# A perceiver kernel on one core: the second cross attention with transposed scores, f32r values and a LayerNorm folded into its weights

## The chip, the cores and the metric

The kernel runs on one core of a Trainium2 chip, as one program that holds a two-layer perceiver. The metric is the device time of one execution in microseconds (us), the median of several. PE is TensorE, DVE VectorE, ACT ScalarE, POOL GpSimd, SP the engine whose queue issues the DMAs.

## What is computed

Sixteen sequences of 64 latent vectors of width 128 (1024 rows) pass two layers. The part that the change touches is the cross attention of layer 1, cut to what matters:

```python
x = x + xattn(ctx_1024, layernorm(x), ln1_w, ln1_b, ln2_w, ln2_b, Wq, Wkv, Wo)

def xattn(ctx, latents, ...):            # ctx (16, 1601, 128), latents (16, 64, 128)
    xn   = layernorm(ctx) * ln1_w + ln1_b
    latn = layernorm(latents) * ln2_w + ln2_b
    q    = latn @ Wq                     # 16 heads of 64
    k, v = split(concat([xn, latn], axis=1) @ Wkv)
    w    = softmax(q k^T / 8)            # (16, 16 heads, 64, 1665)
    return (w v) @ Wo
```

Everything is f32. Kernels of this case compute a product of f32 numbers in two ways. One is TensorE's f32 product, which shows as two records. The other splits each operand into a high half rounded to f32r and a low half (the rest, as f32r), and adds three f32r passes: high by high, high by low, low by high.

## The kernel before, in words

The program runs in stages, one block of instructions after another: the cross attention of layer 0 (tensor names `a_`), the folding of the weights of the second cross attention (`f_`), the rest of layer 0 (`b_`), the second cross attention (`c_`) and the rest of layer 1 (`d_`). A block begins when all engines have ended the one before, and the DMAs of it.

**Folding** (`fold_resampler_weights`, L1064). For each of 16 heads the query and key weights become one 128 by 128 matrix `qk`, the value and output weights one matrix `wvo`. TensorE transposes the raw blocks, then multiplies them, and DVE and ACT copy the results from PSUM. ln2's affine is applied to the latents in the rest of layer 0, ln1's to the context in the attention.

**Rest of layer 0** (`rest_of_layer_0`, L1130). Two rounds (a `Fori`) of four tiles, each tile two sequences. At its end TensorE makes the absorbed queries: in two parts (L1296) eight heads of `qk` by the transposed latents of each tile, which ACT and DVE copy out of PSUM and SP stores in DRAM (`absorbed_queries`, 512 KB a sequence). So 16 heads by 64 latents form 1024 columns a sequence.

**Second cross attention** (`attend`, L114, driven by `cross_attention_1`, L1745). A batch is one sequence: 1665 keys (1601 of context in 12 tiles of 128 and one of 65, and 64 of latents as the fourteenth tile, all side by side in one row) by 1024 queries. It is taken as 8 pairs of heads (128 queries), four pairs to a quad. For each pair the scores come with queries as partitions and keys as columns, in four chunks of up to 512 keys, three f32r passes each (L266). DVE takes the maximum of each chunk from PSUM (L359) and the largest of the four. ACT computes exp of the chunks with that maximum as bias and adds up the rows on the way (L340). TensorE transposes the probabilities (L237), DVE (L369, L373) and ACT (L324) copy them to SBUF, and when a quad is complete they are multiplied by the normalised rows `c_xn` in f32 (L1904, 512 columns). The reciprocal of the sums is spread over 128 partitions by a diagonal that POOL makes (L1918), and TensorE (`norm`). DVE multiplies the values by it; one f32 product per head with `wvo` makes the output of two sequences (L1890), which DVE adds to `x_tok`.

In the course of a batch the next one is prepared: DVE takes the statistics of its context, POOL computes the root (L1827, a power), normalises 13 tiles of rows (L1836), applies ln1's weight and bias (L1843, L1850) and splits the queries into halves (L1820, L1822). TensorE transposes the rows (L1884), ACT takes the high half of the result (L1939) and DVE the low half (L1946). A table places each of these jobs in one of 16 slots of a body of two sequences; every engine works through its list in order and waits on semaphores.

## Time and profile before

| | us |
|---|---|
| median of 3 runs | 2067.46 (2066.22 to 2070.15) |
| the profiled execution | 2070.69 |
| its span in the trace | 2068.9 |
| busy: PE 1746.9, DVE 1276.0, ACT 853.5, POOL 504.4 | 84%, 62%, 41%, 24% |
| second cross attention, between its first and last score | 966.6 |

The profiled execution is 1.8 us longer than its span, since it counts what lies around the first and the last instruction. It is 3.2 us above the median. The granted clock of TensorE, averaged over the span, was 0.909 of full speed.

### The profile page before, as it was taken

Reading aid. Unit: us, or ns where it says so; the run is one execution under the profiler, and the core shown is the slowest. Engines: PE = TensorE matmul, PEld = TensorE weight load, DVE = VectorE, ACT = ScalarE, POOL = GpSimd, SP = SyncE. Lnnn points to the kernel's source line nnn. Section 1 sums busy time; section 2 is a strip of 40 time slices with the busy share of each in tenths; the row PEclk is TensorE's granted clock in tenths of the full one; section 3 lists DMA queues with packets and bytes.
Section 4 is the critical chain, followed back from the end, with each engine's and each line's share of the span. In section 5 each row is a group of like instructions: output and inputs, shape, how many; then the busy total and the mean of one; then the engine's idle time right before and its main releaser. Section 6 shows DMA issues by size and latency. Waiting matters only on the chain. (4 is left out here: it accounts for less than half of the span.)

```text
span 2068.9 us, 33746 instructions
## 1 busy us (share of the span) xinstructions
PE 1746.9 (84%) x11837; PEld 1232.3 (60%) x11837; DVE 1276.0 (62%) x3092; ACT 853.5 (41%) x1895; POOL 504.4 (24%) x684
## 2 busy tenths in 40 slices
PE   5899999999966666428999999999999999999432
PEld 2466666666655555426666666766667666675322
DVE  5566666666736545636666656666666666654467
ACT  2355555565532122114444444444444444443132
POOL 1000001000001010023442344443234444320133
PEclk9699999999977776768999999999999999999765
DMA  4344435444210020040000000000000000000000
GB/s 104 92 105 105 112 81 113 98 112 106 55 42 1 1 81 0 0 152 27 27 11 27 16 26 26 26 10 26 18 23 26 26 26 10 16 1 1 0 5 5
DMA packets 32628, 90.06 MB, mean 44 GB/s; under 512 B 8552, under 2 KB 17424, under 8 KB 32528
## 3 DMA queue, kind: packets, MB, share of 16 engines
q1 hardware_dynamic: 32528, 88.71, 16.0%
q8 instruction: 65, 1.06, 0.2%
q14 instruction: 35, 0.29, 0.0%
HBM read 40.43 MB, written 8.91 MB: 24 GB/s over the span
## 5 line engine op out<-in xcount | busy, mean ns | idle before, releaser
L1904 PE MATMUL c_pv_ps<-c_prob_t,c_xn 128*128 128x512 f32 (+2 forms) x896 | 413.1, 598 | 0.0
L340 ACT ACTIVATE c_prob<-c_score_ps,c_neg_max 128x512 f32<-128x512 f32 (+1 forms) x512 | 304.3, 607 | 60.4 <-PE c_scratch L1890 35.0
L871 DVE TENSOR_REDUCE a_chunk_max<-a_side_ps 128x1 f32<-128x512 f32 (+1 forms) x416 | 260.7, 664 | 109.5 <-PE a_side_ps L692 109.4
L359 DVE TENSOR_REDUCE c_chunk_max<-c_score_ps 128x1 f32<-128x512 f32 (+1 forms) x512 | 290.9, 581 | 38.1 <-PE c_score_ps L266 36.6
L237 PE MATMUL c_turn_ps<-consts,c_prob 128*128 128x128 f32 (+2 forms) x1792 | 285.7, 276 | 5.2 <-DVE c_prob_t L369 4.3
L237 PEld LDWEIGHTS c_turn_ps<-consts,c_prob 128*128 128x128 f32 (+2 forms) x1792 | 212.4, 139 | 89.2 <-issue 32.4
L1904 PEld LDWEIGHTS c_pv_ps<-c_prob_t,c_xn 128*128 128x128 f32 (+2 forms) x896 | 158.4, 191 | 164.6 <-issue 164.5
L373 DVE COPY c_prob_t<-c_turn_ps 65x128 f32<-65x128 f32 (+1 forms) x256 | 61.5, 280 | 300.5 <-PE c_turn_ps L237 300.5
L804 ACT ACTIVATE a_prob<-a_st_ps 128x1024 f32<-128x1024 f32 (+1 forms) x224 | 214.4, 958 | 66.8 <-PE a_st_ps L676 66.8
L266 PE MATMUL c_score_ps<-c_x_hi,c_q_hi 128*128 128x512 f32 (+1 forms) x512 | 218.8, 427 | 2.4 <-ACT c_prob L340 1.6
L266 PE MATMUL c_score_ps<-c_x_hi,c_q_lo 128*128 128x512 f32 (+1 forms) x512 | 188.6, 368 | 0.0
L324 ACT ACTIVATE c_prob_t<-c_turn_ps 128x512 f32<-128x512 f32 x128 | 76.4, 597 | 270.7 <-PE c_turn_ps L237 269.2
L266 PE MATMUL c_score_ps<-c_x_lo,c_q_hi 128*128 128x512 f32 (+1 forms) x512 | 187.6, 366 | 0.0
L369 DVE COPY c_prob_t<-c_turn_ps 128x512 f32<-128x512 f32 x256 | 173.8, 679 | 0.2 <-PE c_turn_ps L237 0.2
L676 PE MATMUL a_st_ps<-a_q_bd,a_stack 100*128 100x256 f32 (+1 forms) x832 | 167.5, 320 | 0.0
L692 PE MATMUL a_side_ps<-a_stack,a_q_bd 96*128 96x512 f32 (+1 forms) x512 | 155.2, 389 | 3.6 <-DVE a_chunk_max L871 1.3
L1913 POOL CAST c_rden_hi<-c_rden 128x4 fp32r<-128x4 f32 x32 | 6.0, 187 | 529.3 <-DVE c_rden L383 529.3
L725 PE MATMUL a_pv_ps<-a_prob,a_val 128*17 128x128 f32 (+1 forms) x3328 | 134.3, 276 | 0.7 <-ACT a_raw L829 0.4
L676 PEld LDWEIGHTS a_st_ps<-a_q_bd,a_stack 100*128 100x128 f32 (+1 forms) x832 | 115.0, 187 | 29.7 <-issue 26.8
L1939 ACT ACTIVATE c_x_hi<-c_scratch 128x512 fp32r<-128x512 f32 x64 | 33.2, 518 | 191.1 <-PE c_scratch L1884 191.1
L725 PEld LDWEIGHTS a_pv_ps<-a_prob,a_val 128*17 128x17 f32 (+1 forms) x3328 | 71.7, 96 | 62.3 <-issue 58.5
L266 PEld LDWEIGHTS c_score_ps<-c_x_hi,c_q_lo 128*128 128x128 f32 x512 | 97.8, 191 | 17.4
(286 smaller groups left out, 2649.9 us busy)
## 6 DMA issues: line engine op xcount, KB each, us to landing
a_stack<-a_k_hi SPq DMA_DIRECT2D x128, 200.1 KB, 4.1
a_stack<-a_k_lo SPq DMA_DIRECT2D x64, 200.1 KB, 4.2
a_ctx<-in_ctx_dram SPq DMA_DIRECT2D x16, 768.0 KB
c_ctx<-in_ctx_dram SPq DMA_DIRECT2D x16, 768.0 KB
absorbed_queries<-b_q_out SPq DMA_DIRECT2D x16, 512.0 KB, 4.7
c_q_raw<-absorbed_queries SPq DMA_DIRECT2D x16, 512.0 KB, 3.3
w<-in_L_ffn_w_dram SPq DMA_DIRECT2D x2, 512.0 KB
f_raw<-in_L_xattn_Wkv_dram SPq DMA_DIRECT2D x2, 512.0 KB, 4.7
```

The costliest lines, as they stand in the source:

```text
L237: last = nc.tensor.transpose(turn_ps[c % 2][0:rows, P * i:P * i + P], prob[(s - 1) % 2][:, col:col + rows], ident)
L266: mm = nc.tensor.matmul(score_ps[:, cols], queries, keys_t[:, cols], start=(i == 0), stop=(i == len(passes) - 1))
L324: nc.scalar.activation(prob_t[u][:, 8:12, P * j:P * j + P], turn_ps[0][:].rearrange("p (t q) -> p t q", t=4), ACT.Copy).then_inc(copied_ac ...
L340: nc.scalar.activation(prob[s % 2][:, cols], score_ps[:, cols], ACT.Exp, bias=neg_max[:, s % 2:s % 2 + 1], accum_out=sums[:, (s // QUAD) % ...
L359: nc.vector.reduce_max(chunk_max[:, s % 2, c:c + 1], score_ps[:, quad_chunk(c, keys)], AX_X).then_inc(chunk_max_done, 1)
L369: last = nc.vector.tensor_copy(prob_t[u][:, 4 * c:4 * c + 4, P * j:P * j + P], turn_ps[c][:].rearrange("p (t q) -> p t q", t=4))
L676: last = nc.tensor.matmul(st_ps[t % 2][0:rows, i, 256 * v:256 * v + 256], stack[:, m, 2 * u + v, col:col + rows], q_bd[m][:, 2 * u + v].re ...
L692: return nc.tensor.matmul(out, q_bd[m][0:ONES_AT, v, 2 * (j % 2):2 * (j % 2) + 2, :].rearrange("p h q -> p (h q)"), stack[0:ONES_AT, m, v, ...
L725: last = nc.tensor.matmul(pv_ps[32 * j:32 * j + V_COLS, 0:P], val[m][0:rows, 2 * s + i, QUAD * u + j, :], prob[t % 3][0:rows, i, P * j:P * ...
L804: nc.scalar.activation(out, scores, ACT.Exp).then_inc(exp_done, 1)
L871: nc.vector.reduce_max(out, rows, AX_X).then_inc(side_taken, 1)
L1904: last = nc.tensor.matmul(lay.own.pv_ps[:], t.xn[m][0:rows, i, :], lay.own.prob_t[u][0:rows, i, :], start=(i == 0), stop=(i == LAT))
```

## The change

- **Folding.** The LayerNorm affines go into the weights. `qk` and `wvo` hold two matrices for each head, one for context keys and one for latent keys. The 16 transposes of the key and value blocks become 16 products of 256 columns with `fold_k` or `fold_v`, and for each head there is one product of 256 columns and two of 128. DVE and ACT share the copies in four banks. Four more small DMAs load the vectors.
- **Rest of layer 0.** The two rounds are written out without the `Fori`. The normalised rows are not copied to `heads_t` by DVE, the next operation reads them where they are. The absorbed queries are made in four parts instead of two, stored in two tensors of the old size.
- **Second cross attention**, written anew. A batch is two octets of eight heads (512 queries), an octet has seven steps of two key tiles: the same 14 tiles, but the latents have their own queries (those folded with their own affine) and columns set apart in the rows. For each key tile the scores come transposed, with keys as partitions and 512 queries as columns, in three f32r passes; the tile of latents has a fourth with one row. Since a maximum over keys can't be taken there, it comes from separate products of one pass with queries as partitions (`max_units_of_c`, 14 to an octet, in two banks, an octet and more ahead); DVE reduces them, and four tiny transposes bring the shift into row 0 of `q_lo`, so that the scores' product subtracts it. ACT takes exp of 128 by 1024 and then writes the high half of the result; DVE, or POOL at steps 1 and 4, the low half. The values are three f32r passes for each key tile with `v_hi` and `v_lo` as weights; POOL splits the values. Column 0 of the rows holds ones, so that row 0 of the result is the sum. The probabilities are not transposed or copied. `norm` is preceded by eight one-row products (`den`), and the output takes 32 products for two sequences instead of 16.
- POOL's list is written out: in even octets high queries, low half, low queries, low half, split values, spread denominators; in odd ones low half, spread denominators, factors (the power), low half, centred rows.

```diff
+                    pe.wait_ge(s.folds, 7)
+                    for n in range(2):
+                        block_n = 2 * (i - 2) + n
+                        fold = fold_k if block_n < PAIRS else fold_v
+                        last = nc.tensor.matmul(ps[i % 4][:, 2 * n:2 * n + 2, :], raw[:, PAIRS + block_n, :], fold[:], start=True, stop=True)
...
+            for h in range(HEADS):
+                if h >= 4:
+                    pe.wait_ge(s.copied if h % 2 == 0 else s.taken, GROUPS // 2 + h // 2 - 1)
+                half, b = slice(64 * (h % 2), 64 * (h % 2) + 64), h // 2
+                nc.tensor.matmul(ps[h % 4][:, 0:2, :], q_turned[half, b, :], kv_turned[half, b], start=True, stop=True)
+                for i in range(2):
+                    last = nc.tensor.matmul(ps[h % 4][:, 2 + i, :], kv_turned[half, PAIRS + b, i, :], raw_o[half, b, :], start=True, stop=True)
...
-                    copy(heads_t[j][:], g.act_t[:, :, :, bass.ds(P * (WIDTH * k + j), P)], s.staged)
...
-                for part in range(2):
+                for part in range(4):
-                            pe.wait_ge(s.q_copied, WIDTH * (2 * k + part) + j - BANK_SETS + 1)
+                            pe.wait_ge(s.q_copied, WIDTH * (4 * k + part) + j - BANK_SETS + 1)
-                            mm = nc.tensor.matmul(ps_c[j % BANK_SETS][:, P * h:P * h + P], g.qk[:, 8 * part + h, :], lat_t[j][:], start=True, stop=True)
+                            mm = nc.tensor.matmul(ps_c[j % BANK_SETS][:, P * h:P * h + P], g.qk[:, 8 * (part % 2) + h, part // 2, :], lat_t[j][:], start=True, stop=True)
...
+                        cp = nc.vector.tensor_copy(g.lat_rows[:, row + b, 1:D], ln_d.out[j][64 * b:64 * b + 64, 1:D])
...
-def attend(nc, g, lay, ctx):
...
+LOW_ON_POOL = (1, 4)
...
+def job_of_c(n, s):
+    b = n // 2
+    if s == 1:
+        return ("lat", n - 1) if n > 0 else None
+    if n % 2 == 0:
+        if s in (0, 2, 3, 4):
+            return ("x_t", {0: 0, 2: 1, 3: 2, 4: 3}[s], b + 1) if b + 1 < BATCH else None
+        return ({5: "den", 6: "norm"}[s], n - 1) if n > 0 else None
+    if s == 0:
+        return ("out", (n - 5) // 4) if n % 4 == 1 and n >= 5 else None
+    return ({2: "den", 4: "norm"}[s], n - 1) if s in (2, 4) else None
...
+def max_units_of_c(n, s):
+    octet, at = divmod(STEPS_C * n + s + 3, STEPS_C)
+    return [("max", octet + 1, 2 * at + i) for i in range(2)] if octet + 1 < OCTETS else []
...
+def first_sides_of_c():
+    return [("max", 0, i) for i in range(UNITS_C)] + [("shift", 0)] + [("max", 1, i) for i in range(6)]
...
+        def low_halves(engine, ops, done, t):
+            engine.wait_ge(hi_done, t + 1)
+            if t >= 3:
+                engine.wait_ge(pv_done, t - 2)
+            for rows, part in ((P, slice(0, 2)),) if t % STEPS_C < STEPS_C - 1 else ((TAIL, slice(0, 1)), (SEQ, slice(1, 2))):
+                last = ops.tensor_tensor(p_lo[t % 3][0:rows, part], prob[t % 2][0:rows, part], p_hi[t % 3][0:rows, part].bitcast(F32), ALU.subtract)
+            last.then_inc(done, 1)
...
+        def centred_rows(engine, ops, b):
+            engine.wait_ge(shift_done, b + 1)
+            if b >= 1:
+                engine.wait_ge(v_low, 2 * b)
+                wait_ready(engine, ("x_t", 3, b - 1))
             for i in range(FULL + 1):
+                rows = tiles[i][0]
+                ops.tensor_scalar(xn[0:rows, i, 1:D], ctx_in[0:rows, i, 1:D], rstd[0:rows, i:i + 1], shift[0:rows, i:i + 1],
+                                  ALU.mult, ALU.add).then_inc(x_done, 1)
...
+            def high_queries(b):
+                m = b % 2
+                pool.wait_ge(q_loaded, 32 * (b + 1))
+                if b >= 2:
+                    pool.wait_ge(scored, STEPS_C * 2 * (b - 1))
+                for i in range(2):
+                    nc.gpsimd.tensor_copy(q_hi[m][:, i], q_raw[:, i]).then_inc(q_split, 1)
+            def low_queries(b):
+                m = b % 2
+                pool.wait_ge(q_split, 4 * b + 2)
+                for i in range(2):
+                    nc.gpsimd.tensor_tensor(q_lo[m][:, i], q_raw[:, i], q_hi[m][:, i].bitcast(F32), ALU.subtract).then_inc(q_split, 1)
+            def split_values(b):
+                m = b % 2
+                pool.wait_ge(x_done, TILES * (b + 1))
+                if b >= 2:
+                    pool.wait_ge(pv_done, STEPS_C * 2 * (b - 1))
+                nc.gpsimd.tensor_copy(v_hi[m][:], xn[:]).then_inc(v_high, 1)
+                pool.wait_ge(v_high, b + 1)
+                for part in (slice(0, 7), slice(7, TILES)):
+                    nc.gpsimd.tensor_tensor(v_lo[m][:, part], xn[:, part], v_hi[m][:, part].bitcast(F32), ALU.subtract).then_inc(v_low, 1)
+            def spread_denominators(n):
+                wait_taken(pool, ("den", n))
+                nc.gpsimd.tensor_copy(rden_hi[:], rden[:]).then_inc(rden_split, 1)
+                pool.wait_ge(rden_split, 2 * n + 1)
+                nc.gpsimd.tensor_tensor(rden_lo[:], rden[:], rden_hi[:].bitcast(F32), ALU.subtract).then_inc(rden_split, 1)
+                pool.wait_ge(rden_split, 2 * n + 2)
+                if n:
+                    wait_ready(pool, ("norm", n - 1))
+                for out, part in ((diag_hi, rden_hi[:].bitcast(F32)), (diag_lo, rden_lo[:])):
+                    nc.gpsimd.tensor_tensor(out[:], ident.unsqueeze(1).broadcast_to([P, QUAD, P]),
...
+            for n in range(OCTETS):
+                t, ahead = STEPS_C * n, n // 2 + (2 if n % 2 else 1)
+                if n % 2 == 0:
+                    if ahead < BATCH:
+                        high_queries(ahead)
+                    low_halves(pool, nc.gpsimd, low_pool, t + LOW_ON_POOL[0])
+                    if ahead < BATCH:
+                        low_queries(ahead)
+                    low_halves(pool, nc.gpsimd, low_pool, t + LOW_ON_POOL[1])
+                    if ahead < BATCH:
+                        split_values(ahead)
+                    if n:
+                        spread_denominators(n - 1)
+                else:
+                    low_halves(pool, nc.gpsimd, low_pool, t + LOW_ON_POOL[0])
+                    spread_denominators(n - 1)
+                    if ahead < BATCH:
+                        factors(ahead)
+                    low_halves(pool, nc.gpsimd, low_pool, t + LOW_ON_POOL[1])
+                    if ahead < BATCH:
+                        centred_rows(pool, nc.gpsimd, ahead)
+            spread_denominators(OCTETS - 1)
...
+                for at, (i, rows, col) in enumerate(step_tiles[s]):
+                    out, keys, which = st_ps[t % 2][0:rows, at, :], slice(col, col + rows), int(i == LAT)
+                    if i == LAT:
+                        nc.tensor.matmul(out, x_hi[m][0:1, keys], q_lo[m][0:1, 0, cols], start=True, stop=False)
+                    nc.tensor.matmul(out, x_hi[m][:, keys], q_hi[m][:, which, cols], start=(i != LAT), stop=False)
+                    nc.tensor.matmul(out, x_lo[m][:, keys], q_hi[m][:, which, cols], start=False, stop=False)
+                    last = nc.tensor.matmul(out, x_hi[m][:, keys], q_lo[m][:, which, cols], start=False, stop=True)
...
+            def weigh(out, t, at, rows, m, i, start, stop):
+                nc.tensor.matmul(out, v_hi[m][0:rows, i, :], p_hi[t % 3][0:rows, at, :], start=start, stop=False)
+                nc.tensor.matmul(out, v_lo[m][0:rows, i, :], p_hi[t % 3][0:rows, at, :], start=False, stop=False)
+                return nc.tensor.matmul(out, v_hi[m][0:rows, i, :], p_lo[t % 3][0:rows, at, :], start=False, stop=stop)
...
+                elif what == "den":
+                    pe.wait_ge(pv_taken, job[1] + 1)
+                    for j in range(QUAD):
+                        for part in (raw_ctx, raw_lat):
+                            last = nc.tensor.matmul(scratch[:, j:j + 1], part[0:1, P * j:P * j + P], ones[0:1, 0:1],
+                                                    start=(part is raw_ctx), stop=(part is raw_lat))
...
+                    for h in range(HEADS):
+                        for i in range(2):
+                            last = nc.tensor.matmul(scratch[:, 0:D], u_t[i][:, h], g.wvo[:, h, i, :],
+                                                    start=(h == 0 and i == 0), stop=(h == HEADS - 1 and i == 1))
...
+                    job = job_of_c(n, s)
+                    scores(n, s)
+                    for side in max_units_of_c(n, s):
+                        side_product(side)
+                    if s == 1:
+                        scratch_job(job)
+                    if n * STEPS_C + s >= 2:
+                        weigh_values(n * STEPS_C + s - 2)
+                    if shift_of_c(n, s):
+                        side_product(shift_of_c(n, s))
+                    if s != 1:
+                        scratch_job(job)
...
+                    nc.scalar.activation(prob[t % 2][:], st_ps[t % 2][:], ACT.Exp).then_inc(exp_done, 1)
...
+                    nc.scalar.activation(p_hi[t % 3][:], prob[t % 2][:], ACT.Copy).then_inc(hi_done, 1)
...
+            for n in range(OCTETS):
+                for s in range(STEPS_C):
+                    t = n * STEPS_C + s
+                    for side in max_units_of_c(n, s):
+                        take_side(side)
+                    if not on_pool(t):
+                        low_halves(dve, nc.vector, low_dve, t)
+                    if shift_of_c(n, s):
+                        take_side(shift_of_c(n, s))
+                    take(job_of_c(n, s))
+                    statistics(n // 2 + 2, tiles_with_statistics(n, s))
+            for job in (("den", OCTETS - 1), ("norm", OCTETS - 1), ("out", BODIES - 1)):
+                take(job)
```

## Rows read from the trace of the kernel before

**Rows 1.** Windows, one per stage: busy us (instructions), PEclk, DMA share, GB/s.
```profile
591.70:616.70 25.00, 14.20 (x89) 12.36 (x89) 7.93 (x19) 1.79 (x3) 0.05 (x1) 0.66 0.24 84
896.50:929.00 32.50, 4.03 (x15) 2.58 (x15) 19.80 (x59) 2.57 (x5) 10.72 (x9) 0.50 0.30 100
929.00:1895.60 966.60, 956.53 (x4659) 655.48 (x4660) 617.84 (x1722) 430.98 (x1233) 375.31 (x512) 0.99 0.06 20
1895.60:1927.10 31.50, 27.07 (x97) 14.14 (x95) 5.67 (x15) 4.74 (x12) 2.42 (x4) 0.95 0.00 0
```

**Rows 2.** Windows, 120 us inside the second cross attention.
```profile
1240.00:1360.00 120.00, 119.91 (x591) 82.12 (x589) 77.77 (x221) 52.76 (x153) 50.16 (x68) 1.00 0.07 22
```

**Rows 3.** Timeline of TensorE there: start us, us, instruction, count.
```profile
1300.29 0.39 PE L266 MATMUL c_score_ps<-c_x_hi,c_q_lo 128*128 128x512 f32 x1
1300.52 0.60 PE L237 MATMUL c_turn_ps<-consts,c_prob 128*128 128x128 f32 x4
...
1301.65 0.22 PE L266 MATMUL c_score_ps<-c_x_hi,c_q_hi 128*128 128x130 f32 x1
1301.71 0.27 PE L266 MATMUL c_score_ps<-c_x_lo,c_q_hi 128*128 128x130 f32 x1
...
1302.64 3.60 PE L1904 MATMUL c_pv_ps<-c_prob_t,c_xn 128*128 128x512 f32 x8
```

**Rows 4.** Groups there, forms apart: count | busy us, mean ns.
```profile
L359 DVE TENSOR_REDUCE c_chunk_max<-c_score_ps 128x1 f32<-128x512 f32 x331 | 223.0, 680 | 23.3 <-PE c_score_ps L266 23.3
...
L1836 POOL TENSOR_SCALAR c_ctx<-c_ctx,c_rstd,c_shift 128x128 f32<-128x128 f32 x168 | 72.3, 448 | 3.0 <-POOL c_shift L1829 3.0
...
L1827 POOL TENSOR_TENSOR c_rstd<-c_rstd,c_half 128x13 f32<-128x13 f32 x14 | 34.1, 2436 | 31.3 <-DVE c_shift L1980 31.3
L1822 POOL TENSOR_TENSOR c_q_lo<-c_q_raw,c_q_hi 128x1024 fp32r<-128x1024 f32 x14 | 33.0, 2356 | 1.1
...
L1918 POOL TENSOR_TENSOR c_diag_hi<-consts,c_rden_hi 128x512 fp32r<-128x512 f32 x28 | 29.1, 1041 | 2.2
...
L1820 POOL CAST c_q_hi<-c_q_raw 128x1024 fp32r<-128x1024 f32 x14 | 14.5, 1036 | 0.0
```

**Rows 5.** Groups of us 750 to 1000: instructions of 1024 columns.
```profile
L1429 DVE TENSOR_TENSOR b_prob_t<-b_sc 128x1024 f32<-128x1024 f32 x4 | 4.9, 1224 | 10.3 <-ACT b_sc L1332 10.3
...
L1317 ACT ACTIVATE b_sc<-b_sc 128x1024 f32<-128x1024 f32 x4 | 4.2, 1057 | 27.6 <-DVE b_sc L1407 27.3
```

**Rows 6.** Timeline of VectorE, start of the stage.
```profile
914.23 0.68 DVE L1843 TENSOR_TENSOR c_ctx<-c_ctx,c_ln_w 128x512 f32<-128x512 f32 x1
915.55 1.52 DVE L1843 TENSOR_TENSOR c_ctx<-c_ctx,c_ln_w 128x512 f32<-128x512 f32 x1
917.10 2.71 DVE L1850 TENSOR_TENSOR c_xn<-c_ctx,c_ln_b 128x512 f32<-128x512 f32 x1
```

**Rows 7.** Timeline of GpSimd, the same moments.
```profile
914.97 1.55 POOL L1820 CAST c_q_hi<-c_q_raw 128x1024 fp32r<-128x1024 f32 x1 [3.57 <-DMA c_q_raw<-absorbed_queries]
916.60 2.67 POOL L1822 TENSOR_TENSOR c_q_lo<-c_q_raw,c_q_hi 128x1024 fp32r<-128x1024 f32 x1
```

**Rows 8.** Windows around one stop of TensorE: PEclk is the third from last.
```profile
958.70:962.50 3.80, 0.06 (x2) 0.04 (x1) 0.99 (x4) 1.93 (x5) 3.72 (x6) 0.88 0.00 0
962.50:968.40 5.90, 5.90 (x21) 5.07 (x22) 3.06 (x6) 1.61 (x5) 5.68 (x7) 0.50 0.00 0
```

**Rows 9.** Timeline of TensorE: absorbed queries, first scores of the stage, output projection.
```profile
737.46 15.56 PE L1296 MATMUL b_ps_c<-b_lat_t,qk 128*128 128x128 f32 x128
...
928.96 0.77 PE L266 MATMUL c_score_ps<-c_x_hi,c_q_hi 128*128 128x512 f32 x1 [0.79 <-DVE c_x_lo L1946]
...
1922.09 3.81 PE L1890 MATMUL c_scratch<-wvo,c_u_t 128*128 128x128 f32 x32 [0.88 <-DVE c_u_t L2015]
```

**Rows 10.** Timeline: weight folding, its first products and its last copy.
```profile
599.40 4.36 PE L1095 MATMUL f_ps<-consts,f_raw 128*128 128x128 f32 x20 [10.12 <-DMA f_raw_o<-in_L_xattn_Wo_dram]
...
615.53 0.41 DVE L1127 COPY wvo<-f_ps 128x256 f32<-128x256 f32 x1
```

1008 lines of the change are left out of this document (425 added, 583 removed).

## The prediction

> **What bounds the kernel now.** I read the windows by stage first [rows 1]. The second cross attention holds 966.6 us of the 2068.9 between its first and last score, and TensorE is busy for 956.5 of them. 120 us from its middle [rows 2] leave no doubt: TensorE 119.91 busy at full clock, DVE 77.8, ACT 52.8, POOL 50.2. So here the order of TensorE's instructions sets the time, and every other engine has slack. The stage has 16 batches: a batch costs 60.0 us, half a batch 30.0. The stages around it are the opposite: TensorE 4.0 of 32.5 us at the start of the attention [rows 1].
>
> The timeline gives TensorE's prices by the distance of starts, since the durations overlap: an f32r pass of 512 columns 0.23 us (1300.29 to 1300.52), one of 130 columns 0.06 to 0.11; an f32 product of 512 columns and 128 rows 3.60 / 4 = 0.90 in a run of values, two records each, with its tail; I take 0.86 [rows 3]. An f32 product of 128 columns is two records, 3.81 / 32 = 0.12 a record with the tail, 15.56 / 128 = 0.122 in the queries; I take 0.114 without the tail [rows 9]. The groups by form give DVE's maximum of 512 (0.680), POOL's row (0.448), power (2.436), subtraction (2.356) and cast (1.036) of 1024 and diagonal (1.041) [rows 4]. A subtraction of 1024 from SBUF takes DVE 1.224, ACT copies 1024 in 1.057 [rows 5].
>
> **TensorE, an octet against half a batch.** After: 13 tiles with three passes for scores, one for the latents with four, and as many for values, 40 + 3 + 42 = 85 by 0.23 = 19.55. Maxima 12 by 0.23 and 8 small ones by 0.11 = 3.64. Shift 0.44. Transposes of the next rows 0.76, `norm` two passes 0.46, `den` 16 small records by 0.11 = 1.76, outputs 64 records in four octets by 0.114 = 1.82. Sum 28.4, with 0.3 for gaps 28.7, a batch 57.4. The same sum over the old order gives 29.7 against 30.0 measured. So if TensorE never waited, a batch would fall by 2.6 us: the transposes of probabilities (56 records) pay for cheaper values and more scores work. The gain is small, so waits decide.
>
> **The wait I see.** POOL's list is in fixed order. In an even octet it takes low half of step 4, then `split_values`, then `spread_denominators`, and TensorE's `norm` at the end of step 6 waits for the latter. From TensorE's start of step 4, it gets to `norm` after 3.85 (six score and six value passes 2.76, two maxima 0.46, shift 0.44, one transpose 0.19), 4.98 (2.76, 0.46, `den` 1.76) and 3.45 (13 passes 3.0, two maxima): 12.3. POOL has: scores, exp and high half 3.85 (six passes 1.4, twice 1.06 on ACT and the hand-overs 0.35), low half 2.36, cast of 14 tiles 1.036 by 1.75 = 1.81, subtraction 2.356 by 1.75 = 4.12, two small instructions and two diagonals 2.6, gaps 0.25: 15.1 in all. TensorE stands for 2.8 us in each batch. In odd octets the same spread comes right behind a low half, and centred rows, 13 by 0.448 = 5.8, come last: no wait, except that the first transpose of the next octet finds them late by some 0.45.
>
> **The wait I can't see in full.** At the start of the attention DVE's product of two SBUF operands took 0.68 alone, and 1.52 and 2.71 while POOL was in a cast and a subtraction [rows 6]; these took POOL 1.55 and 2.67 instead of 1.036 and 2.356 [rows 7, 4]. In the steady state before, DVE has almost no such instruction: it reads PSUM. After, it takes ten low halves a batch, 12.2 us alone, and POOL stands at 36 to 38 us a batch. Where they meet, one waits for the other: the low halves of steps 5 and 6 meet `split_values`, which delays the diagonals by one or two low halves, 1.2 to 2.45. I take the upper, 2.4, since both steps fall into the 6 us of the split. From below it is 0 (if they don't meet), from above DVE's low halves each wait for a whole POOL instruction of up to 4.12 / 2, and TensorE, which needs them two steps later (8 us), follows: +5.
> The Trainium skill, page "SBUF — State Buffer", section "Who interferes with whom", has it that a DVE instruction with two SBUF inputs contends with a GpSimd instruction that reads SBUF, and that who issues second is blocked for the whole instruction. By that rule, the trace agrees: 2.71 for 0.68 [rows 6]. The sum by it is the one that I take, by a rule of no contention it would be 2.4 a batch less.
>
> **The clock.** After a stop of 3.8 us the granted clock is 0.50, the lower level of 1.2 GHz, for 5.9 us, then back at full [rows 8]; that costs 5.9 / 2 = 2.95, with the transition 3.4. Stops in the steady state were too short or none. A stop of 5.2 (2.8 + 2.4) is of the long kind when it falls together; I charge half of the batches, 1.7. Bounds 0 and 3.4.
>
> Batch: 57.4 + 2.8 + 2.4 + 0.45 + 1.7 = 64.75. Sixteen: 1036.0. Off come 13.8 for the first and the last batch, where nothing is spread or nothing split (2.8 + 2.4 + 1.7 each), and 13.8 for work that lies outside (no values in the first two steps 2.8, first `den` and `norm` 2.2, last transposes 1.5, last values, `den` and outputs in the tail 7.3); 9.4 is added for the low clock, as it was before: 0.99 on the average of 966.6 us [rows 1] is 9.7, with the stage before at 0.50 and one stop [rows 8]. That is 1017.8 against 966.6: **+51.2**.
>
> **Around it.**
> - Absorbed queries: twice 64 products more, 14.3 each without the tail (8 products 1.79; 15.56 with it [rows 9]): +28.6. TensorE has a wait here only for copies of 1.06 on two engines per eight products of 1.79, hidden. Waits for `heads_t` go: -4.7. At the end of the block 9.3 us now pass from the last copy (887.2) to the next block (896.52 [rows 1]) for stores; the parts are spread over 57 us, not 28: -4, between 0 and -9.
> - Folding: products start at 599.40 and the last copy begins at 615.53 [rows 10], 16 us. At full clock TensorE has now 16 products of 256 columns (0.43 each, 6.9) and for each head 512 columns (0.86, 13.8); before it had 16 transposes (1.8) and 256 columns for each head (7.3). That is 11.6 more at full clock, 17.6 at the stage's 0.66 [rows 1]. The copies double in size but are shared by two engines; four small DMAs stand ahead of the weights' loads. A stage with more work has less of it in the slow stretch, so I take +13.5, range +8 to +30 (all at 0.5, and a DMA behind the small ones late by 7).
> - Start of the attention: before, 32.5 us [rows 1]. Weight and bias on the rows (0.68 each, one of 1.52 and 2.71 [rows 6]) go, 5.1. But before the first scores DVE has now the statistics of the second batch (13 times 0.28 and the means, 4.2) and 20 maxima by 0.68 [rows 4], 13.6, and the shift 0.8: 18.6 - 5.1 = +13.5, first scores 45.9 after the block's start where they were 32.4 (928.96 [rows 9]); and POOL's splits of the queries meet DVE's centred rows, which now stand beside them: +3.8 (one cast 1.04 and one subtraction 2.36, and gaps). Sum **+17.3** (+8 to +25).
> - Tail: after the last score there were four chunks of transposes, copies and values; now exp, high and low half 4.9, two steps of values 2.1, copies 1.2, `den` 1.8, POOL's diagonals 2.6, `norm` and product 2.0, 64 records instead of 32 (3.81 [rows 9]) 7.3, the addition 0.8. 31.5 [rows 1] becomes 22.7: -8.8.
>
> Sum around: 28.6 - 4.7 - 4 + 13.5 + 17.3 - 8.8 = +41.9. The rest (layer 0's attention, rest of layer 1) stays: 0.
>
> Total 51.2 + 41.9 = +93.1 on the profiled execution's 2070.69: 2163.8; it lies 3.2 over the median of the runs, so **2160**.
>
> **Rivals.** (1) Only the stop by POOL's order exists, 2.8 a batch, without contention or low clock: a batch 57.4 + 0.45 + 2.8 = 60.65; by 16, less 5.6 and 13.8 and with 9.4, is 960.4, and 2070.7 - 6.2 + 41.9 - 3.2 = 2103, slower. For: the steady low halves are spread over the octet. Against: rows 6. Chance 0.20. (2) The other side: TensorE never waits in the steady state, 57.4 a batch, because POOL is early enough (the low half of step 4 is ready sooner than I sum, or the step is longer). 918.4 - 13.8 + 9.4 = 914.0, 52.6 less; with +41.9 around and 3.2 off 2057, faster. It decides from a stop under 0.75 us a batch (10.7 us are left between 2057 and 2067.5, for 14 batches). For: POOL was busy only 25 of 60 us before [rows 2]. Against: 15.1 stands to 12.3. Chance 0.15. (3) DVE starves behind POOL's back-to-back instructions, and the lag of two steps does not cover it: 5 a batch more, 14 by 5 = 70, 2230. For: 2.71 for a 0.68. Against: 12.2 and 37 of a batch of 57 still fit one behind the other. Chance 0.12. The forecast 0.50; something else 0.03. That the change does not do what it says is no case here: the work on TensorE is in the diff line by line.
>
> **The range.** The forecast's own: the folding -6 or +17, the clock 24 either way (1.7 by 14), contention -34 (2.4 by 14) or +36; not all at once, 2115 to 2215. The range over the cases is 2080 to 2220: it holds (1) and the lower half of (3), and leaves out (2) and the rest, 0.2. A difference of 0.2% (4 us) is about what a measurement of this kernel can tell from none. Faster is (2) and a little of (1), 0.17; same 0.03; slower 0.80.
>
> **What the changed profile would show.** Right: a TensorE idle of 3 to 5 us ahead of `norm` in even octets with POOL's diagonal as releaser, none in odd ones; DVE's low halves with a mean above 1.3 and single ones above 2; POOL's split above 4.12; PEclk below 1.0 in windows inside the attention; busy TensorE of 57 us a batch; 28 to 30 us for the queries a round; first score some 46 us after the block's start. Wrong: windows of the attention with TensorE at 100% (rival 2), or DVE's low halves at 1.22 (rival 1), or idles with DVE as releaser (rival 3).

## The result

The changed kernel takes 2175.69 us (2163.65 to 2184.75), the kernel before 2067.10: a ratio of 1.052 with a 95% interval of 1.047 to 1.057. The forecast was 2160, 2080 to 2220, slower with a chance of 0.80. The profiled execution has 2178.6 us and a span of 2176.8, which is 107.9 more than before.

The windows by stage of the changed kernel (busy us of PE, PEld, DVE, ACT and POOL, granted clock, DMA share, GB/s), to be read beside [rows 1]:

```profile
592.50:625.70 33.20, 19.39 (x136) 17.18 (x136) 10.66 (x28) 8.26 (x21) 0.00 (x0) 0.76 0.21 64
625.70:921.90 296.20, 193.87 (x1477) 174.38 (x1477) 148.03 (x395) 71.16 (x101) 24.61 (x41) 0.77 0.15 57
921.90:971.55 49.65, 18.84 (x44) 10.02 (x45) 33.11 (x98) 3.35 (x5) 26.27 (x30) 0.50 0.28 93
971.55:2009.60 1038.05, 978.97 (x4657) 758.70 (x4656) 685.16 (x1233) 533.72 (x630) 567.21 (x515) 0.95 0.07 26
2009.60:2034.50 24.90, 17.60 (x102) 14.90 (x100) 3.51 (x7) 3.42 (x6) 2.43 (x4) 0.79 0.00 0
```

| | before | after | more | forecast |
|---|---|---|---|---|
| folding | 25.0 | 33.2 | 8.2 | 13.5 |
| rest of layer 0 | 279.8 | 296.2 | 16.4 | 19.9 |
| start to first score | 32.4 | 49.65 | 17.2 | 17.3 |
| first to last score | 966.6 | 1038.05 | 71.4 | 51.2 |
| tail | 31.5 | 24.9 | -6.6 | -8.8 |
| layer 0's attention, rest of layer 1 | | | 1.3 | 0 |

The stages around came out nearly as summed. The main part is 20 us longer than forecast, and how it is made up differs more than that number shows. For it I take one stretch in each kernel, the 13 batches from the fourth shift to the thirtieth (the shift is L1741, one an octet). TensorE's waits in that stretch of the changed kernel, in all, times, longest:

```profile
PE c_side_ps L1741 <- DVE c_chunk_max L1930: 32.7, 13, 3.8
PE c_scratch L1761 <- DVE c_x_lo L1944: 13.8, 13, 1.1
PE c_scratch L1807 <- POOL c_diag_lo L1667: 1.9, 4, 0.6
PE c_scratch L1791 <- DVE c_x_lo L1944: 0.7, 2, 0.3
```

And the windows row of the stretch:

```profile
1056.11:1914.62 858.51, 811.12 (x3869) 629.27 (x3870) 581.75 (x1069) 438.11 (x520) 488.96 (x455) 0.95 0.08 27
```

858.5 / 13 = 66.0 us a batch. TensorE is idle for 858.5 - 811.1 = 47.4 us, 3.65 a batch (the list has 1.7 more, since it counts the stop that ends where the stretch begins). From the clock records of the same trace 82 us are at the lower level, each worth half, 3.15 a batch (PEclk 0.95 says the same, 0.05 by 66 = 3.3). What is left, 59.2, is TensorE's work at full clock. **The stop that I had forecast before `norm` (L1807, released by POOL's diagonals) is 1.9 us in 13 batches. The real one, 2.5 on the mean and once a batch, is before the shift, and released by DVE's maxima.** The timeline around one of them shows why (start, duration, instruction, and in brackets what ended the idle time before it):

```profile
1172.66 4.73 POOL L1645 TENSOR_TENSOR c_q_lo<-c_q_raw,c_q_hi 128x1024 fp32r<-128x1024 f32 x2
...
1174.31 1.29 DVE L1930 TENSOR_REDUCE c_chunk_max<-c_side_ps 128x1 f32<-128x512 f32 x2 [3.54 <-PE c_side_ps L1736]
...
1177.42 0.34 SPq L1599 DMA_DIRECT2D c_q_raw<-queries_for_context  x1
...
1177.80 0.42 SPq L1599 DMA_DIRECT2D c_q_raw<-queries_for_latents  x1
...
1178.27 0.43 SPq L1592 DMA_DIRECT2D c_ctx<-in_ctx_dram  x1
...
1178.74 0.41 SPq L1594 DMA_DIRECT2D c_ctx<-in_ctx_dram  x1
...
1184.94 0.49 DVE L1897 BATCH_NORM_STATS2 c_stats<-c_ctx 128x6 f32<-128x128 f32 x2 [2.73 <-DMA c_ctx<-in_ctx_dram]
1185.34 0.30 DVE L1901 BATCH_NORM_AGGREGATE c_mean_var<-c_stats 128x2 f32<-128x6 f32 x2
1185.56 1.27 DVE L1930 TENSOR_REDUCE c_chunk_max<-c_side_ps 128x1 f32<-128x512 f32 x2
...
1186.28 0.60 PE L1741 MATMUL c_side_ps<-consts,c_neg_max 128*1 128x128 f32 x4 [2.19 <-DVE c_chunk_max L1930]
```

POOL ends the low halves of the queries at 1177.4. Only then SP issues the loads of the next queries, and behind them, at 1178.27, that of the context, whose buffer had been free since the rows were centred (1165.6, below). It has landed by 1184.9, when DVE starts on it. DVE's list holds the statistics at this place, so DVE stands 2.73 us for it, and the maxima behind it are late. TensorE waits for these maxima's values before the shift.

The second stop, 1.06 a batch, comes from the centred rows. POOL's timeline in the odd octet:

```profile
1157.83 7.85 POOL L1620 TENSOR_SCALAR c_xn<-c_ctx,c_rstd,c_shift 128x127 f32<-128x127 f32 x13
1165.63 0.28 POOL L1622 COPY c_xn<-lat_rows 64x128 f32<-64x128 f32 x1
```

And the groups of these instructions over the stretch, forms apart (count, busy us, mean ns):

```profile
L1586 DVE TENSOR_TENSOR c_p_lo<-c_prob,c_p_hi 128x1024 fp32r<-128x1024 f32 x104 | 169.1, 1626 | 39.3 <-ACT c_p_hi L1858 39.3
...
L1586 POOL TENSOR_TENSOR c_p_lo<-c_prob,c_p_hi 128x1024 fp32r<-128x1024 f32 x52 | 124.1, 2386 | 305.1 <-ACT c_p_hi L1858 305.1
...
L1620 POOL TENSOR_SCALAR c_xn<-c_ctx,c_rstd,c_shift 128x127 f32<-128x127 f32 x156 | 96.0, 631 | 0.0
```

On the mean a row takes 0.631 where it took 0.448 [rows 4], and DVE's low half 1.626 where such a subtraction took 1.224 [rows 5]. POOL's low half, 2.386, is hardly longer (2.356 [rows 4]). But these means mix two kinds. The line of the rows in the same stretch (count: shortest, median, longest in ns):

```profile
L1620 POOL TENSOR_SCALAR c_xn<-c_ctx,c_rstd,c_shift x169: 455/465/1488, 1089.3 to 1896.9; 128x127 f32<-128x127 f32 x156, 65x127 f32<-65x127 f32 x13
```

Most rows take what they took before, and a few take two or three times as much: of the 156 rows of 128 partitions 117 are at 0.47, 26 near 0.96 and 13 near 1.48, so two and one to a batch. In the same way 68 of DVE's 104 low halves take less than 1.3 and 32 over 2. Of the 36 above 1.3, 26 run beside POOL's halves of the queries and 10 beside its split of the values.

### The profile page after: what moved, and what is told of

Its sections match the earlier page's. It is cut to its first block and busy times, and to the rows that moved or that the text cites. A ratio compares the mean times of both kernels' runs of the same rounds, so it can differ in the third digit from the quotient of the medians.

```text
span 2176.8 us, 32509 instructions
## 1 busy us (share of the span) xinstructions
PE 1807.2 (83%) x12173; PEld 1374.7 (63%) x12173; DVE 1357.9 (62%) x2644; ACT 973.3 (45%) x1312; POOL 712.1 (33%) x708
## 5 line engine op out<-in xcount | busy, mean ns | idle before, releaser
L1930 DVE TENSOR_REDUCE c_chunk_max<-c_side_ps 128x1 f32<-128x512 f32 (+1 forms) x448 | 271.7, 644 | 154.2 <-PE c_side_ps L1736 153.8
L1849 ACT ACTIVATE c_prob<-c_st_ps 128x1024 f32<-128x1024 f32 x192 | 197.0, 1026 | 344.7 <-PE c_st_ps L1721 344.6
L1586 DVE TENSOR_TENSOR c_p_lo<-c_prob,c_p_hi 128x1024 fp32r<-128x1024 f32 (+1 forms) x192 | 249.9, 1314 | 91.4 <-ACT c_p_hi L1858 62.9
L1858 ACT ACTIVATE c_p_hi<-c_prob 128x1024 fp32r<-128x1024 f32 x192 | 203.6, 1060 | 6.1
L1719 PE MATMUL c_st_ps<-c_q_hi,c_x_hi 128*128 128x512 f32 (+1 forms) x448 | 194.7, 434 | 0.0
L1721 PE MATMUL c_st_ps<-c_q_lo,c_x_hi 128*128 128x512 f32 (+1 forms) x448 | 187.6, 419 | 0.0
L1720 PE MATMUL c_st_ps<-c_q_hi,c_x_lo 128*128 128x512 f32 (+1 forms) x448 | 186.3, 416 | 0.0
L1736 PE MATMUL c_side_ps<-c_x_hi,c_q_hi 128*128 128x512 f32 (+2 forms) x640 | 170.5, 375 | 6.1 <-DVE c_chunk_max L1930 5.6
L1761 PE MATMUL c_pv_ps<-c_p_hi,c_v_hi 128*128 128x512 f32 (+1 forms) x416 | 174.5, 420 | 0.1
L1762 PE MATMUL c_pv_ps<-c_p_hi,c_v_lo 128*128 128x512 f32 (+1 forms) x416 | 166.8, 401 | 0.0
L1736 PEld LDWEIGHTS c_side_ps<-c_x_hi,c_q_hi 128*128 128x128 f32 x640 | 116.2, 207 | 37.3 <-DVE c_chunk_max L1930 12.9
```

The costliest lines, as they stand in the source:

```text
L1586: last = ops.tensor_tensor(p_lo[t % 3][0:rows, part], prob[t % 2][0:rows, part], p_hi[t % 3][0:rows, part].bitcast(F32), ALU.subtract)
L1719: nc.tensor.matmul(out, x_hi[m][:, keys], q_hi[m][:, which, cols], start=(i != LAT), stop=False)
L1720: nc.tensor.matmul(out, x_lo[m][:, keys], q_hi[m][:, which, cols], start=False, stop=False)
L1721: last = nc.tensor.matmul(out, x_hi[m][:, keys], q_lo[m][:, which, cols], start=False, stop=True)
L1736: return nc.tensor.matmul(out, q_hi[m][:, which, first:first + P], x_hi[m][:, cols], start=True, stop=True)
L1849: nc.scalar.activation(prob[t % 2][:], st_ps[t % 2][:], ACT.Exp).then_inc(exp_done, 1)
```

## The experiments

Theory Q: SP's queue makes the stop before the shift. Theory P, my forecast's: the fixed order on POOL makes it. Theory C: the rows make the stop of 1.06. Theory W, which came up after e1 to e4: the narrow `den` makes the clock fall. A "spell" is a time without a break at the lower of the two clocks (1.2 instead of 2.4 GHz, granted 0.50). Each kernel has three rounds beside the kernel before on the same chip. "Batch" is the same stretch (fourth shift to thirtieth) over 13, "stops" the time in it in which TensorE is idle, "clock" half of its time at the lower level, "rest" what is left, all for one batch. For the kernel before, which has no shift, it is the 840 us from 1000 to 1840, 14 batches.

| | median us | ratio, interval | batch | stops | clock | rest |
|---|---|---|---|---|---|---|
| before | 2067 | 1 | 60.0 | 0 | 0 | 60.0 |
| changed | 2175.7 | 1.052 (1.047 to 1.057) | 66.0 | 3.65 | 3.15 | 59.2 |
| e1 | 2146.9 | 1.039 (1.037 to 1.041) | 64.6 | 2.9 | 2.2 | 59.4 |
| e2 | 2219.9 | 1.072 (1.067 to 1.078) | 69.5 | 5.6 | 4.3 | 59.5 |
| e3 | 2214.7 | 1.072 (1.070 to 1.074) | 68.6 | 5.6 | 5.2 | 57.8 |
| e4 | 2130.4 | 1.030 (1.028 to 1.032) | 63.1 | 1.5 | 2.1 | 59.5 |
| e5 | 2125.1 | 1.029 (1.026 to 1.031) | 62.9 | 1.8 | 1.7 | 59.3 |
| e6 | 2116.3 | 1.023 (1.021 to 1.025) | 62.2 | 1.1 | 1.3 | 59.8 |
| e7 | 2163.3 | 1.048 (1.043 to 1.052) | 66.2 | 3.7 | 3.3 | 59.2 |
| e8 | 2141.2 | 1.036 (1.033 to 1.038) | 63.5 | 1.2 | 3.15 | 59.1 |
| e9 | 2098.1 | 1.015 (1.014 to 1.017) | 61.1 | 1.3 | 0.7 | 59.2 |
| e10 | 2123.6 | 1.028 (1.026 to 1.030) | 62.9 | 2.9 | 1.05 | 58.9 |
| e11 | 2172.7 | 1.052 (1.050 to 1.053) | 65.6 | 4.6 | 2.2 | 58.8 |
| e12 | 2099.8 | 1.017 (1.015 to 1.019) | 61.1 | 1.3 | 0.7 | 59.1 |

(In e3 29 us of the stops lie in spells of low clock, so that half of them, 1.1 a batch, is taken off twice and the rest comes out too small; in e11 it is 0.1. The other differences in the rest are not explained.)

**e1: context load first.**

```diff
             for b in range(1, BATCH):
-                sp.wait_ge(q_split, 4 * b)
-                load_q(b)
                 sp.wait_ge(x_done, TILES * b)
                 load_ctx(b)
+                sp.wait_ge(q_split, 4 * b)
+                load_q(b)
```

> The only edit: SP loads the context of the next batch as soon as its buffer is free, ahead of the queries. Theory Q (SP's queue holds the context load behind POOL's low halves of the queries, DVE then stands for it at its first statistics with the maxima queued behind, and TensorE stands before the shift): TensorE's stop before the shift in even octets (2.5 us) goes; POOL's diagonals, which had been covered by that stop, are then late by about 1.1 us before norm. Main part 20 to 50 us shorter, the whole 2125 to 2155. Rival P (POOL's fixed order alone makes the stop, and the place where TensorE stands is by chance): the stop only moves to norm at its full 2.5 us, 2165 to 2180.

2146.9. TensorE's waits in e1:

```profile
PE c_scratch L1807 <- POOL c_diag_lo L1667: 22.4, 13, 2.8
PE c_scratch L1761 <- DVE c_x_lo L1944: 13.9, 13, 1.1
```

The stop before the shift is gone to the last tenth, and the stop before `norm` is there with 1.7 us a batch: theory Q, and behind it my old one. The order on POOL was late all the time, and TensorE's stop for SP's load had given it the time. POOL's chain in one even octet of e1 (the split of the values 5.24 us, `den` long done):

```profile
1172.06 2.40 POOL L1586 TENSOR_TENSOR c_p_lo<-c_prob,c_p_hi 128x1024 fp32r<-128x1024 f32 x1 [7.09 <-ACT c_p_hi L1858]
...
1174.41 1.68 POOL L1652 CAST c_v_hi<-c_xn 128x1792 fp32r<-128x1792 f32 x1
...
1176.16 5.24 POOL L1655 TENSOR_TENSOR c_v_lo<-c_xn,c_v_hi 128x896 fp32r<-128x896 f32 x2
...
1181.98 1.04 POOL L1667 TENSOR_TENSOR c_diag_hi<-consts,c_rden_hi 128x512 fp32r<-128x512 f32 x1 [0.17 <-POOL c_rden_lo L1662]
...
1182.98 1.49 POOL L1667 TENSOR_TENSOR c_diag_lo<-consts,c_rden_lo 128x512 fp32r<-128x512 f32 x1
...
1184.61 0.48 PE L1807 MATMUL c_scratch<-c_diag_hi,c_ones_r 128*128 128x512 f32 x1 [1.45 <-POOL c_diag_lo L1667]
```

**e2: diagonals ahead of the split of the values.**

```diff
-                    if ahead < BATCH:
-                        split_values(ahead)
                     if n:
                         spread_denominators(n - 1)
+                    if ahead < BATCH:
+                        split_values(ahead)
```

> The only edit: in even octets POOL spreads the denominators before it splits the values. Theory Q: TensorE still stands 2.5 us before the shift; only the short gap before norm (some 0.3) goes: 2165 to 2176. Rival P: the POOL order is the cause, the stop of 2.8 and 2.4 a batch goes, 2100 or less.

2219.9: neither theory had expected a loss of 44 against the changed kernel. The waits of POOL in its stretch:

```profile
POOL c_rden_hi L1660 <- DVE c_rden L1953: 162.9, 26, 10.7
```

And those of TensorE:

```profile
PE c_side_ps L1741 <- DVE c_chunk_max L1930: 39.8, 13, 4.5
PE c_scratch L1761 <- DVE c_x_lo L1944: 13.7, 13, 1.1
PE c_side_ps L1736 <- DVE c_chunk_max L1930: 9.3, 7, 1.7
PE c_scratch L1812 <- DVE c_u_t L1957: 8.8, 6, 1.9
```

POOL now stands 162.9 us in 26 times, up to 10.7, for the reciprocals, with the split queued behind it. The split falls into the next octet and meets the work there: stops of 1.7 and 1.9 appear before maxima (L1736) and before the output product (L1812). The stop before the shift is 3.1. So the order on POOL was not the cause of the stop, and to change it alone costs.

**e3: rows early.** In odd octets DVE takes the low half of step 4.

```diff
     def on_pool(t):
-        return t % STEPS_C in LOW_ON_POOL
+        return t % STEPS_C == LOW_ON_POOL[0] or t % (2 * STEPS_C) == LOW_ON_POOL[1]
...
                     if ahead < BATCH:
                         factors(ahead)
-                    low_halves(pool, nc.gpsimd, low_pool, t + LOW_ON_POOL[1])
```

> The only edit: in odd octets DVE, not POOL, takes the low half of step 4, so that POOL's centred rows begin some 4 us earlier. Theory C (the stop of 1.05 us at step 1 of even octets comes from centred rows late by their meeting with DVE's low halves, and it draws one spell of low clock of 3.4 us, 1.7 us lost): both go, 14 by 2.75 = 38 us, 2130 to 2145. Rival: the clock falls for the other stop, then only 15 us: 2160. Rival D: DVE has no room for the twelfth low half and its maxima are late: no gain or a loss.

2214.7, a miss in sign. TensorE's waits:

```profile
PE c_side_ps L1740 <- DVE c_chunk_max L1929: 78.0, 13, 6.6
```

The stop of 1.06 is gone as theory C says. But the one before the shift is 6.0 instead of 2.5: SP's load still waits for the low halves of the queries, TensorE without its first stop and its low clock comes to the shift some 2.7 sooner, and these low halves took 5.73 us instead of 4.73 in the octets compared. That the 3.5 more (6.0 - 2.5) come from the two is argued from these numbers, not tried by itself. Together with the load ahead (e4, e5) the same edit gains.

**e4: all three, and e5: e1 and e3 without e2.**

> The three edits together. If the stops (2.5 and 1.05, with 0.3 before norm) and all low spells behind them (3.0 us lost a batch) go, a batch costs 59.6 and the main part is 14 by 6.8 = 95 shorter: 2080. If POOL or DVE then becomes the next bound, 2100 to 2130.

> The edits of e1 and e3, without that of e2 (POOL again splits the values ahead of the diagonals). Theory: the order on POOL is what stands before norm (1.7 us a batch in e1), the order of e2 is what stands before the output product and the maxima in e4 (1.5 a batch). Then here the stop of 1.06 and its low clock are gone, the stop before norm is 1.7 to 2.8: 2115 to 2147. Rival: DVE's twelfth low half, not POOL's order, made e4's stops, then both kinds appear: above 2147.

2130.4, where 2080 was hoped for and 2100 to 2130 expected if another engine became the bound, and 2125.1, within its range. TensorE's waits in e4:

```profile
PE c_scratch L1811 <- DVE c_u_t L1956: 9.9, 6, 1.9
PE c_side_ps L1735 <- DVE c_chunk_max L1929: 9.2, 7, 1.7
```

And in e5:

```profile
PE c_scratch L1806 <- POOL c_diag_lo L1667: 23.5, 13, 2.7
```

So Q and C hold, and P as far as the second stop goes: each order has the stop that was expected of it, and the 1.06 and the 2.5 are gone in both. But e4 has 2.1 us a batch of low clock with only 1.5 of stops, in which I had expected none. Eight of its 15 spells in the stretch have no stop ahead, but `den`.

**e6, e9: `den` wide, `den` full.** The sixteen records of `den` have one row and one column. Both kernels stand on e4. e6 gives the records 128 columns, of which only the first is read. e9 gives them 128 rows too: all rows of the raw values meet a matrix `one_row` whose first row is ones and whose others are zero, so that the sums stay. The line that changes:

```diff
-  last = nc.tensor.matmul(scratch[:, j:j + 1], part[0:1, P * j:P * j + P], ones[0:1, 0:1],
+  last = nc.tensor.matmul(scratch[:, P * j:P * j + P], part[0:1, P * j:P * j + P], ones[0:1, 0:P],   # e6
+  last = nc.tensor.matmul(scratch[:, P * j:P * j + P], part[:, P * j:P * j + P], one_row[:],         # e9
```

> e4 with the den products 128 columns wide instead of one (same number of records, same place; only the first column of each is used). In e4 nine of the seventeen low spells begin 1 to 3 us after den, with no idle of TensorE ahead of them. Theory W (the narrow den counts as a pause for the clock): these go, e4's 2.1 us lost a batch fall to about 1, 2130 becomes 2115. Rival: the clock falls because of the idle times or of the work as a whole: 2125 to 2135, spells stay.

> e6 with the den products on 128 rows as well (all rows of the raw values by a matrix whose first row is ones and whose others are zero; the same sums, the same 16 records of 0.112 us). Theory W (the clock falls after den because den gives the array almost nothing to do): the spells that still follow den in e6 go, the loss falls from 1.3 us a batch to 0.5 or less: 2116 becomes 2100 to 2108. Rival: den is where spells are seen because the work before it (small maxima, transposes) is thin; then no change, 2113 to 2120.

2116.3 and 2098.1. The windows of e4 around one `den`, which runs from 1421.7 to 1423.5 (the granted clock is the third number from the end):

```profile
1421.50:1424.50 3.00, 3.00 (x22) 2.30 (x20) 2.00 (x6) 0.55 (x1) 0.44 (x3) 1.00 0.00 0
1424.50:1427.90 3.40, 3.40 (x8) 2.17 (x9) 0.94 (x2) 1.34 (x3) 3.40 (x3) 0.50 0.00 0
1427.90:1433.00 5.10, 5.10 (x23) 4.13 (x23) 4.53 (x3) 2.93 (x4) 4.87 (x3) 1.00 0.00 0
```

Those of e9 around one, from 1415.0 to 1416.8:

```profile
1414.80:1417.80 3.00, 3.00 (x22) 2.38 (x20) 2.10 (x7) 0.71 (x1) 0.39 (x2) 1.00 0.00 0
1417.80:1421.20 3.40, 3.40 (x15) 2.53 (x15) 1.29 (x3) 2.22 (x4) 3.37 (x3) 1.00 0.00 0
```

In both TensorE is busy for all of the 3.00 us, without a stop ahead. In e4 the clock falls to 0.50 for the next 3.4 us, in e9 it does not. In the 13 batches e4 has eight spells with `den` and no stop ahead, e6 seven (and one with a stop, where e4 had seven), e9 none, and four behind stops. So e6 came out at the time that theory W gave it (2115) but not by its mechanism: seven of the eight spells behind `den` stayed, and what it gained came from the spells behind stops. With rows and columns together theory W holds: in e9 the spells with `den` alone are gone, and in e12, which has the same `den`, there is none either. e9 is 32 us faster than e4 by a `den` that takes the same time and gives the same sums; of the 2.0 us a batch between the two the clock has 1.4. That the kernel's busy share tells nothing of it is the point: e4's TensorE "worked".

**e11: the changed kernel with the full `den` alone.**

> The changed kernel with that den alone, every wait as it is. It has 3.2 us of low clock lost a batch; of its 26 spells most follow the stop of 1.06 and some den. Theory W: the spells behind den go (8 of 26), 2175 becomes 2155 to 2168; those behind the stop stay. If the narrow den had made the clock ready to fall for the stop too, more: 2135 to 2150. Rival: the spells stay, 2170 to 2180.

2172.7, within the changed kernel's spread and outside both ranges of theory W; it is the time of the rival, by which the spells would stay. But they went: none in the stretch has only `den` ahead any more (six had), and the clock costs 2.2 instead of 3.15. What took the gain is in the waits:

```profile
PE c_side_ps L1746 <- DVE c_chunk_max L1936: 44.1, 13, 4.4
PE c_scratch L1766 <- DVE c_x_lo L1950: 13.8, 13, 1.1
```

The stop before the shift is 3.4 instead of 2.5: TensorE came sooner and stood longer for the same load; that this is the whole reason is argued from the rows. A gain ahead of a stop that another engine's chain sets is eaten by it.

**e8: POOL without most of the values' low halves, on e1.**

```diff
+                    width = part if b < 2 else slice(part.start, part.start + 1)
-                    nc.gpsimd.tensor_tensor(v_lo[m][:, part], xn[:, part], v_hi[m][:, part].bitcast(F32), ALU.subtract)...
+                    nc.gpsimd.tensor_tensor(v_lo[m][:, width], xn[:, width], v_hi[m][:, width].bitcast(F32), ALU.subtract)...
```

> e1, but from the third batch on POOL computes the low half of the values for 2 of the 14 tiles only. Left out: that part of the values' precision. POOL is 3.5 us shorter in an even octet. Theory: the stop before norm (1.7) goes, the 1.06 stays since it comes from the centred rows in the odd octet: 2147 less 14 by 1.7 to 2.3: 2115 to 2123. Rival contention: DVE's low halves are the late ones; then their mean falls to 1.23 and the stop of 1.06 goes too, 2090 to 2105.

2141.2, only 6 less than e1, both expectations missed. The stop before `norm` is gone and the 1.06 stays, as expected. What the stop gave, 1.7 a batch, the clock took back for more than half: 3.15 against 2.2, 12 of 18 spells behind `den`. And the split is not what DVE's low halves meet most (10 of the 36 long ones above): over the whole run their mean (1024 columns) is 1.591 with the short split, 1.704 in e1, 1.599 in the changed kernel, against 1.224 alone.

**e7: two of four parts of the queries.** It leaves out the queries folded for the latents, and stores each part twice, so that the bytes written stay. The main lines of the edit:

```diff
-                for part in range(4):
+                for part in range(2):
...
-                            sp.dma_start((dram.q1, dram.q2)[part // 2][batch:batch + 1, :, cols]...
+                            for q in (dram.q1, dram.q2):
+                                sp.dma_start(q[batch:batch + 1, :, cols]...
```

> The changed kernel with two of the four parts of the absorbed queries; each part is stored in both tensors, so that the bytes written stay. Left out: the queries folded for the latents. By the forecast's term (64 products more in each of two rounds, 14.3 us each) it is 28.6 shorter than the changed kernel: 2147. Rival: the copies to SBUF and the stores, not the products, set the pace of the parts: a gain under 20.

2163.3, 12.4 less than the changed kernel by the medians and 20.6 by the profiled executions (2158.0 for 2178.6), where 28.6 were expected. In the traces each round of queries is 14.3 shorter, the term to the tenth. TensorE's first instruction in the attention of the changed kernel:

```profile
942.21 1.09 PE L1791 MATMUL c_scratch<-consts,c_xn 128*128 128x128 f32 x4 [26.26 <-DVE c_xn L1622]
```

And in e7:

```profile
918.35 0.87 PE L1792 MATMUL c_scratch<-consts,c_xn 128*128 128x128 f32 x3 [34.49 <-DVE c_xn L1623]
```

Its idle time before it is 8.2 longer in e7: the same bytes are stored in half the time, and the block ends with the last store. The products' price and the stores' cover are both real, 28.6 - 8.2 = 20.4. That the medians show less lies within the spreads: the changed kernel's runs go from 2163.7 to 2184.8, those of e7 from 2156.6 to 2175.1.

**e10, e12: the two edits around.** The folding's four vectors are loaded behind the weights, and the statistics of the second batch come behind the first octet's maxima; e10 on e5 with the full `den`, e12 on e9.

> e5 (context load first, rows early) with the full den, the four vectors of the folding loaded behind the weights (1.9 us), and the statistics of the second batch behind the first octet's maxima (3.5 us sooner to the first score). Stop before norm 1.8 a batch stays. By the theories: 2125 less 1.9, less 3.5, less 14 by 1.2 of low clock: 2100 to 2106. It is not expected to reach the kernel before, since TensorE alone needs 59.3 us a batch where the old order took 60.0, and the stages around cost 35 more.

> e9 (context first, diagonals first, rows early, full den) with the two edits around the attention that e10 has: the folding's four vectors loaded behind the weights, and the second batch's statistics behind the first octet's maxima. In e10 the first score came 2.0 us sooner after the block's start and the folding's first product 2.0 us sooner. If the main part is e9's 958.5, the whole is 2094; it stays above the kernel before, since the stages around cost more than the 8 us that e9's main part is below it. Rival: the later start of POOL's rows for the second batch delays the first octets, then 2096 to 2100.

2123.6, a miss (2100 to 2106 were expected), and 2099.8, at the end of its rival's range. e10 is where it is for the reason of e11, one place on:

```profile
PE c_scratch L1812 <- POOL c_diag_lo L1669: 38.3, 13, 3.0
```

2.9 us a batch before `norm` instead of e5's 1.8: POOL's order bounds it, and the clock's gain (1.7 to 1.05) is eaten. e12 is not faster than e9: its first score comes 2.4 us sooner (969.1 for 971.5), and from there to the last score it takes 3.3 longer (961.8 for 958.5). That POOL's later rows do this, as the rival had it, was not tried. e9 is the fastest of the changed order:

```profile
971.50:1929.90 958.40, 938.94 (x4656) 735.78 (x4655) 694.86 (x1249) 532.70 (x630) 554.60 (x499) 0.99 0.08 27
```

Its 958.4 from first to last score are 8 less than the 966.6 before [rows 1], but the stages around cost some 36 (the changed kernel's in the table above, 36.5), so no version here beats the kernel before.

## Why the prediction was right, and where it was not

- **Slower, about 5%**: right, and for the reason given first: TensorE's own work hardly falls, so waits and the stages around decide.
- **"A batch 57.4" if TensorE never waits**: mis-sized. It measures 59.2, and 58.9 to 59.8 in the others once the double count is put back. The terms are there (pass 0.232 for 0.23, `den` 1.8, output 7.1 per two batches), but the sum lacks the changes of kind. The changed kernel's timeline, starts:

```profile
1138.91 0.48 PE L1719 MATMUL c_st_ps<-c_q_hi,c_x_hi 128*128 128x512 f32 x1
1139.23 0.40 PE L1720 MATMUL c_st_ps<-c_q_hi,c_x_lo 128*128 128x512 f32 x1
1139.47 0.40 PE L1721 MATMUL c_st_ps<-c_q_lo,c_x_hi 128*128 128x512 f32 x1
...
1141.83 0.50 PE L1761 MATMUL c_pv_ps<-c_p_hi,c_v_hi 65*128 65x512 f32 x1
```

  From the first pass after an f32 product to the second there are 0.32 (1138.91 to 1139.23), then 0.24; from the first on a tile of 65 keys to the second 0.33, then 0.23. That is 0.1 for each change. In e5's 13 batches at full clock some 22 second passes of 512 columns a batch start late, 2.1 us in all; the sum had 0.6 for all gaps of a batch. That takes rival 2 away: even without a stop the main part gains only (60.0 - 59.2) by 16 = 13.
- **"TensorE stands for 2.8 us in each batch" before `norm`**: the step that failed, by place. In the changed kernel it stands only 0.15 there (1.9 in 13 batches), and 2.5 before the shift, for maxima behind a context load that SP held behind the queries' halves. I had gone through POOL's list and not through SP's, though the load's wait was in the code. The stop I summed exists: e1 shows 1.7, e10 2.9. (POOL's terms in that sum give 15.0, not 15.1, so 2.7 and not 2.8; nothing hangs on it.)
- **"+2.4" for DVE's low halves that meet the split**: not on this path. The meeting is real (means of 1.626 for 1.224, and 0.631 for 0.448 on POOL), but it acts elsewhere, on the rows in the odd octets: 7.85 us for the 13 where 5.8 were summed. The split itself is hardly touched there (two halves of 2.1, 4.2 where 4.12 were summed); it is in e1 that it takes 5.24. The 0.45 forecast for the first transpose became the stop of 1.06 behind it. The Trainium skill ("SBUF — State Buffer", section "Who interferes with whom") says that a DVE instruction with two SBUF inputs contends with a GpSimd instruction that reads SBUF; the trace agrees with that, three rows of a batch being long (0.96, 0.96 and 1.48) and the other nine at 0.47. That ACT never waits on anyone, as the Trainium skill says in the same section, agrees with ACT's 1.06 for 1024 columns before [rows 5] and 1.02 to 1.07 after.
- **The clock, 1.7 a batch**: 3.15. I charged it to one long stop in half of the batches. Of 23 spells 17 stand behind a stop, 11 of them behind one of 1.06, and 6 behind `den`, whose work had one row and one column.
- By terms: work +1.8, stops 3.65 for 5.65, clock +1.45, together +1.3 a batch or 20 us over 16: the difference between 2160 and the measured 2176 and the 5 us by which the stages around came out lower. That the forecast is only 16 us off is luck in part: the stops were summed 2.0 a batch too long, and the two other terms were too small by more than that.
- Around: the start 17.2 for 17.3. (The "some 46 us" that I gave as a sign leaves out the 3.8 of the same sum; with it 49.7, and 49.65 is measured.) The folding 8.2 for 13.5: the products by head take 9.2 (614.99 to 624.23) where 13.8 were summed, and the clock of the stage rose from 0.66 to 0.76; against that the first product comes 3.1 later after the last instruction of the stage before (11.7 us for 8.6), of which the four small loads make 2.0 (9.8 in e10 and e12, where they stand behind the weights). The rest of layer 0 16.4 for 19.9: the products cost what was summed (29.86 for 15.56 a round), and the end of the block, from the last product to the next block, took 4.4 less (6.0 for 10.4) where 4 were summed; instead of the 4.7 summed for the waits on `heads_t`, 4.6 went ahead of the attention of the first round and 4.4 ahead of that of the second. The tail -6.6 for -8.8: the last outputs took 9.55 instead of 7.3, at a lower clock (0.79 over the tail).

Of the rivals, (1) is refuted by the changed profile's 3.15 of low clock a batch and by the place of the stop, (2) by the 59.2, and (3) has its engine right (DVE late), but DVE waits for a DMA there, not for POOL.

## What to carry to other kernels

Write down every queue's list, SP's too, and ask of each load how long its buffer has been free when it is issued: here 12 us. When a stop is found, look for the next chain that it covers before counting its whole length as a gain: of 2.5 us here 1.7 came back at another place, and a faster clock ahead of a stop gave nothing. And when TensorE's clock falls though it is never idle, look at what its instructions feed it.
